# Leaving out the counting semaphore instructions of ScalarE and VectorE in a graph-network kernel

## The reference

```python
# block 0: two graph convolutions with degree norms
h = x * norm_src[:, None] @ W ; agg = segment_sum(h[src], dst) ; agg * norm_dst[:, None] + b
# block 1: concat([x, mean over neighbours]) @ W.T + b
# block 2: two SAGE layers  h @ W_self + mean_neighbours(h) @ W_neigh + b, 128 -> 256 -> 128, relu between
# block 3: messages = gelu([h[src], h[dst], w] @ We1 + be1) @ We2 + be2 ; summed by dst
#          layernorm(h + gelu([h, agg] @ Wu1 + bu1) @ Wu2 + bu2)
```

## Time and profile before

| what | value |
|---|---|
| median of 3 runs | 5151.64 us (5151.11 to 5152.08) |
| the profiled execution's span | 6457.2 us, 132161 instructions |
| TensorE matmul busy | 4407.5 us (68%) |
| VectorE busy | 3589.5 us (56%) |
| ScalarE busy | 3052.6 us (47%) |
| GpSimd busy | 3067.8 us (48%) |
| mean granted TensorE clock | 0.838 of full speed |

### The profile page before, as it was taken

One profiled execution on the slowest core, in us unless ns is written; L12 is line 12 of the kernel. 1 busy time (PEld: TensorE's weight loads), 2 busy tenths in 40 slices (PEclk: granted clock), 3 DMA queues, 4 the chain that ended last, 5 costly groups with the idle time before them and its releaser, 6 DMA issues. The chain is left out here.

```text
span 6457.2 us, 132161 instructions
## 1 busy us (share of the span) xinstructions
PE 4407.5 (68%) x23072; PEld 3228.9 (50%) x23073; DVE 3589.5 (56%) x12501; ACT 3052.6 (47%) x6864; POOL 3067.8 (48%) x3248
## 2 busy tenths in 40 slices
PE   7755555677657877577758999777771566666557
PEld 2333333566656655444436777566661444444345
DVE  9865555444436655466645665466661445455446
ACT  7533333444435555455545665355550334344335
POOL 0154445455545553545535555355545545554541
PEclk9877787777778998899989999899995767777778
DMA  0022222444434444466656787567762444444444
GB/s 18 10 62 66 66 67 72 128 153 154 146 110 149 152 141 135 158 211 215 215 170 214 241 250 242 169 227 231 235 226 86 133 127 141 131 140 133 130 130 140
DMA packets 613683, 956.80 MB, mean 148 GB/s; under 512 B 100096, under 2 KB 255888, under 8 KB 613584
## 3 DMA queue, kind: packets, MB, share of 16 engines
q1 hardware_dynamic: 494848, 746.65, 34.7%
q0 software_dynamic: 100672, 181.64, 11.8%
q10 hardware_dynamic: 18064, 27.47, 1.2%
HBM read 517.00 MB, written 438.38 MB: 148 GB/s over the span
## 5 line engine op out<-in xcount | busy, mean ns | idle before, releaser
L1045 PE MATMUL banks<-M,OH 128*128 x7840 | 1323.0, 319 | 654.8 <-issue 597.2
L588 POOL DMA_INDIRECT M<-table_a,six x1176 | 1117.8, 950 | 903.2 <-PE banks L1045 357.4
L1045 PEld LDWEIGHTS banks<-M,OH 128*128 128x128 f32 x7840 | 1148.7, 215 | 758.3 <-issue 739.2
L681 ACT ACTIVATE AG<-banks x1176 | 635.0, 591 | 1240.0 <-remote 954.3
L588 POOL DMA_INDIRECT M<-table_b,six x784 | 767.6, 979 | 627.0 <-PE banks L1042 208.5
L578 POOL DMA_INDIRECT edges_by_block<-pack,pos_i x392 | 376.5, 961 | 679.7 <-DVE pos_i L1325 558.7
L588 POOL DMA_INDIRECT M<-table_pairs,six x392 | 393.2, 1003 | 572.7 <-DVE ES L1581 451.3
L1441 DVE TENSOR_TENSOR OH<-banks,dstrel 128x1024 f32<-128x1024 f32 x392 | 478.3, 1221 | 221.7 <-remote 190.6
L681 ACT ACTIVATE HT<-banks 128x512 f32<-128x512 f32 x588 | 348.4, 593 | 513.2 <-remote 416.4
L699 ACT ACTIVATE HO<-H,BI,SC 128x128 f32 (+1 forms) x1176 | 485.3, 485 | 133.8 <-issue 73.4
L681 ACT ACTIVATE T<-banks 128x512 f32<-128x512 f32 (+1 forms) x686 | 355.0, 532 | 312.6 <-remote 124.3
(11 more groups left out here) (319 smaller groups left out, 8716.4 us busy)
## 6 DMA issues: line engine op xcount, KB each, us to landing
XZ<-state SPq DMA_DIRECT2D x490, 256.0 KB
table_a<-T SPq DMA_DIRECT2D x294, 256.0 KB
state<-T SPq DMA_DIRECT2D x294, 256.0 KB
state<-H SPq DMA_DIRECT2D x196, 256.0 KB
own_products<-T SPq DMA_DIRECT2D x98, 512.0 KB
table_pairs<-T SPq DMA_DIRECT2D x98, 512.0 KB
M<-messages SPq DMA_DIRECT2D x98, 512.0 KB
XZ<-in_x SPq DMA_DIRECT2D x194, 256.0 KB
```

The costliest lines, as they stand in the source:

```text
L588: nc.gpsimd.indirect_dma_start(out=M[:, slot, :], out_offset=None, in_=table, in_offset=bass.IndirectOffsetOnAxis(ap=idx, axis=0)).then_in ...
L681: return nc.scalar.activation(dst_, src_, ACT.Copy)
L1045: last = mm(banks[:, ds(sums_at[k], P)], OH[:, b * US + k, :], source[:, ds(rows_at[k], P)], start=False, stop=False, skip_group_check=True)
```

## The change

`stand(act)` is left out at all 14 places, and `stand(dve)` at ten of 14, all but those in (`variances0`, `spread`, and `stats` and `variances` of `walked`). Nothing else is touched; SyncE's and GpSimd's stay. The core of the diff:

```diff
                     if d == 3:
                         need(act, st[b], turns(3, "st", i))
-                    stand(act)
                     for j in range(Q4):
...
                     act.wait_ge(s_var, g + (at(d, "var") + 1))
                     need(act, free[0], g + free[1] - 1)
-                    stand(act)
                     nc.scalar.activation(SD[:, b, :], MV[:, b, :, 1], ACT.Sqrt, bias=epsc[:, 0:1]).then_inc(s_sd, 1)
...
                     if d == 5:
                         need(act, sh[b], turns(d, "sh", i))
-                    stand(act)
                     copy(HT[:, b, :], ps[3] if d == 0 else pt).then_inc(s_ht, 1)
...
                     need(act, ev_act, w + WINS * ph)
-                    stand(act)
                     copy(AG[:, ds(spot[2], W4)], banks[:, ds(spot[0], W4)]).then_inc(ev_first, 1)
...
                 act.wait_ge(s_es, c + 1)
-                stand(act)
                 nc.scalar.activation(ES[:, b, :], ES[:, b, :], ACT.Gelu).then_inc(s_gl, 1)
...
                 need(dve, s_scat[b], i * (16 * CH))
-                stand(dve)
                 v.tensor_copy(pack[b][:, :, :], edge4[:, ds(g * CH, CH), :])
...
                 dve.wait_ge(s_own, g + 1)
                 need(dve, sh[b], turns(3, "sh", i))
-                stand(dve)
                 v.tensor_copy(T12[:, b, 1, :], ps[6]).then_inc(s_ob, 1)
...
                 dve.wait_ge(s_mma, g + (at(4, "mma") + 1))
                 need(dve, s_mm, g + (at(4, "mm") - 1))
-                stand(dve)
                 v.tensor_tensor(H[:, b, 0, :], ps[5], Z[:, b, :], ALU.add)
```

## The result

The changed kernel took 5106.4 us (median of 4 runs, 5101.1 to 5111.0) against 5151.4 before: ratio 0.9915, interval 0.9901 to 0.9929, so 45 us less. Forecast were 5132 (20 less) and a range of 5080 to 5160. The direction and the range held; the size was off by a factor of more than two.

What follows compares the result with a forecast made beforehand. Walk 2 was taken to be bound by a circle through several engines, none full; 0.20 us a turn over 90 to 98 turns, 0 elsewhere (fills, walks 0 and 4: 0 to 1), took 5151.6 to 5132 us; range 5080 to 5160.

Steps and rivals of the forecast that it cites:

- Gaps: Walk 2: MV to SD 0.19 to 0.11 us, product to T 0.25 to 0.15 and 0.18 to 0.03 in alternate turns.
- Walk 2's term: Walk 2: 0.12 us at T plus 0.08 at SD saved a turn, 18 to 20 us over 90 to 98 turns.
- the circle: Walk 2: SD, HT, product, T, H, ST, MV and back to SD, 7.02 us a turn, every gap paid in full.
- Walk 5 is paced by VectorE: Walk 5: VectorE busy 7.83 of 8.08 us, so leaving out its counting instruction in `final` gains 0.
- The loads: Walk 5's table loads: hoisting them gives at most 11.5 us, and with VectorE back to back, 0.
- Walks 1 and 4: Walk 1: TensorE is full and covers gaps, 0; walk 4, with walk 0 and the pipeline fills: 0 to 1 us.
- the rival of more circles: Walks 0, 1 and 4 also have gaps on their path: much faster, 5085 to 5110 us, centre 5100; chance 0.21.
- The slower rival: Walk 5's T and walk 2's HT: an instruction holding its own wait loses overlap; 5173 us, chance 0.09.
- its own signs of being wrong: Walk 2's turn stays at 7.0 with smaller gaps, walk 0, 1 or 4 shortens, or walk 5 changes at all.

Runs made afterwards that it cites:

- e2: The kernel before with only ScalarE's counting instructions left out, VectorE's kept; 5124.3 us, ratio 0.9957.
- e3: The kernel before with only VectorE's ten counting instructions left out, ScalarE's kept; 5121.9 us, ratio 0.9959.
- e10: The kernel before with a second counting instruction ahead of walk 2's square root and its copy of the second product; 5176.9 us, ratio 1.0052.
- e1: The kernel before, unchanged, timed against itself as a yardstick; 5153.6 us, ratio 1.0013.
- e4: The kernel before with the counting instructions left out in walk 2 alone, on both engines; 5111.2 us, ratio 0.9934.
- e8: The changed kernel, but with ScalarE's counting instructions kept in walk 5; 5100.7 us, ratio 0.9902 to the kernel before.
- e9: The kernel before with four spare 128x128 products a turn on TensorE in walk 2, ahead of the transposes; 5124.4 us, ratio 0.9955.
- e7: The kernel before with counting instructions left out in walk 5 only, ahead of the square root and the two gelus; 5161.8 us, ratio 1.0023.
- e6: The kernel before with ScalarE's counting instructions left out in walk 4 alone; 5141.7 us, ratio 0.9978.

## Why the prediction came out as it did

**Gaps: right.** The three gaps came out at 0.11, 0.13 and 0.04 for 0.11, 0.15 and 0.03, and the median turn fell by 0.20 as summed; 98 turns give some 20 us. Leaving out half (e2, e3) moves the gaps of that half alone and by the same amounts, and doubling (e10) adds 0.07 to 0.10 to each. It is the counting instruction between the wait and the tensor instruction that costs. The sentence of the Trainium skill, "VectorE: DVE Perf Modes", section "The DRAIN you can't avoid", that a semaphore costs nothing extra, is on copies each with its semaphore; it does not carry over to an instruction of its own that only counts, which cost 0.08 to 0.14 here.

**Walk 2's term: mis-sized, 20 for 38.** The forecast took a turn of 7.01 and its TensorE at full clock, and read the circle from that turn. It was one of the turns without a fall of the clock. One turn in seven had the product at 3.1 to 3.5 us. Shorter gaps leave TensorE idle for less at a stretch (medians, worked out from the traces, of 0.92 and 1.50 us before the transposes in the changed kernel's two kinds of turn, 1.16 and 1.61 in e1's), and the falls go from 13 to 2: 17 us by the product alone. The falls follow the gaps in both directions: 21 with the gaps longer (e10), 7 and 8 with half of them shorter (e2, e3), 2 to 4 with all shorter (e4, e8 and the change). That the fallen clock costs this much is shown by e9, which leaves every gap and takes the falls away. Why these few tenths of a microsecond make such a difference is not shown. The Trainium skill, "TensorE: Matmul & The Clock Gate", has a section "HAM oscillation — how this bites in real kernels" on a clock that falls again and again in a kernel whose TensorE waits for DMA. The trace agrees in the fall, 0.50 for 3 us, but the waits here are for other engines, 1.0 to 1.6 us before the transposes.

**"Walk 5 is paced by VectorE": wrong, and with it the 0 there.** The stretch of 8.08 us held six gathers where a turn needs eight. GpSimd had stood still for 11.8 us just before it, and VectorE was working off gathers made earlier. In an undisturbed execution a turn takes 10.4 us, which is eight gathers of 1.0 and their 0.30. The turns of the earlier trace rows gave 15.1 in the mean, disturbed (1461 us over the 97 steps from the first OH to the last, which the forecast calls 98 turns); their median, worked out from the same trace, is 10.5 and would have said so. The cost of that misreading: +14 us that the forecast had at 0. The loads were hoisted and gained nothing, as forecast, but for another reason than VectorE's load: ScalarE only waited longer elsewhere. With the three counting instructions of e7 gone, VectorE's one-hots fall elsewhere against the gathers, and more gathers start in the first half of an OH. Those three also make the square root and the gelus start sooner after their waits; no run set that apart from the hoist, so that it is the hoist is argued and not shown.

How a VectorE instruction lengthens a gather is in the rows (0.95 to 1.64 us beside OH<-lane,dstrel). The kernel itself has the comparison: line 1441 makes OH in every walk, in the same shape, but in walks 3 and 5 from two operands in SBUF (lane, dstrel) and in the others with one of them in PSUM (banks, dstrel). In walk 2 of the changed kernel a gather that starts 0.50 us into OH takes its plain time:

```profile
2208.78 1.23 DVE L1422 TENSOR_TENSOR OH<-banks,dstrel 128x1024 f32<-128x1024 f32 x1
...
2209.28 0.95 POOL L588 DMA_INDIRECT M<-table_a,six  x1 [1.70 <-PE banks L1031]
```

In walk 3 of e1 one that starts 0.26 us into it takes 1.79:

```profile
2832.58 1.23 DVE L1444 TENSOR_TENSOR OH<-lane,dstrel 128x1024 f32<-128x1024 f32 x1 [0.26 <-DVE XZ L1566]
2832.84 1.79 POOL L591 DMA_INDIRECT M<-table_b,six  x1 [0.30 <-issue]
```

Worked out from the thirteen traces, of gathers that start 0.1 us or more into OH and at least 0.15 before its end: the 3745 of walks 0, 1, 2 and 4 take 0.94 to 0.98 us wherever they start, and the 1603 of walks 3 and 5 all end 0.81 to 0.85 us after OH's end, whenever they started. So the gather makes next to no way until OH is done, and that only where both operands are in SBUF. The Trainium skill, "SBUF — State Buffer", says that VectorE and GpSimd share a pair of ports, held for a whole instruction by whichever comes first, among them a VectorE instruction with two SBUF inputs against a GpSimd one that reads SBUF. The traces agree with that: the hold hangs on the operand, and the 12 gathers of walks 3 and 5 that start up to 0.1 us ahead of OH take 0.94 to 1.00, as the first comer would. That it is these ports is the page's statement; the traces show the hold and what it hangs on.

**Walks 1 and 4: missed, some −6 and −8.** The forecast had them at 0, or 0 to 1; they stood under the rival of more circles. Walk 1's loss goes with ScalarE's instructions (e2, e8, after); e6 bears walk 4 out at −11, with its drift as large.

**The slower rival: its mechanism is refuted.** T in `final` still starts 0.78 after XZ, and HT 0.24 after SD.

The parts, in us by the stages' lengths: walk 2 −38, walk 4 −8, walk 1 −6, walk 5 +14, together −38, against −45 measured with an interval of −37 to −51. What is left is of the size of the control's 7. The two traces of e1 and of the changed kernel by themselves add up to −46: walk 2 −38, walk 4 −19, walk 1 −4, walk 5 +16, the rest −2; so what the means leave out is mostly walk 4, of whose 19 its drift may make more than half. The total hides errors of opposite sign: walk 2 gave nearly twice its term, and walk 5, which the forecast had at 0, took a third of that back; without its loss the time would be near 5092, still in the range. By its own signs of being wrong (walk 1 or 4 shortens, walk 5 changes at all) the forecast missed these stages, though its number held.

**Open.** Why OH moves against the gathers in e7, when VectorE doesn't wait for SD at SC (idle 0.0 there in e1 and in the changed kernel), is not settled; nor what makes walk 4 drift between 670 and 689 with the same code, nor what decides in which turn the clock falls. No run put OH's operand of walk 5 into PSUM or moved OH in its list, which the last reading suggests. Leaving out the instructions ahead of ST and MV, each with 0.15 in the circle, wasn't tried.

## What to carry to other kernels

In this kernel an instruction that only counts, put between a wait and the work, costs 0.07 to 0.14 us where the wait ends last, and nothing where the sequencer runs ahead; read the gap between the releaser's end and the start. When reading a stage from a disturbed trace, take the median turn and not the cleanest, check that it holds all of a turn's work (eight gathers, not six), and compare the mean with the median: the difference is rare events such as a fallen clock. Idle time of TensorE cost twice in walk 2, once as a gap and once by the clock, so spare products in a gap may pay. And look at what a gather runs beside: an operand moved to PSUM may free it.

## What the hardware did that I had not expected

Four spare products a turn made the kernel 24 us faster (ratio 0.9955), because TensorE's granted clock no longer fell to half. Gathers took 0.94 us alone and up to 1.93 us when they started 0.1 us or more into a VectorE comparison with both operands in SBUF, always ending 0.81 to 0.85 us after it; beside the same comparison with one operand in PSUM they took 0.94 to 0.98. Walk 5's length took two values, 1062 to 1069 and 1075 to 1080, by nothing but the counting instructions of ScalarE in it, of which those ahead of the square root and the gelus are enough.
